# Two-layer transformer kernel: in the second layer's rounds the small steps stand behind the scores and maxima, directly ahead of the value products

## What is computed

```python
x = layernorm(x + L0_attn(x))   # 8 heads of 128, 2 key/value groups from a latent of 32, causal
x = layernorm(x + L0_ffn(x))    # silu(gate)*up, operands quantised to FP4 in blocks of 16
x = layernorm(x + L1_attn(x))   # 16 heads of 8, 4 key/value groups, not causal
x = layernorm(x + L1_ffn(x))    # 8 experts, softmax gate, gates under 0.1 dropped
# L1_attn
q = (x @ Wq.T + bq).reshape(b, n, G, hpg, HD); k, v = ...
scores = einsum('bqghd,bkgd->bghqk', q, k) / sqrt(8)
y = einsum('bghqk,bkgd->bqghd', softmax(scores), v) @ Wo.T + bo
```

## Time and profile before

| | us |
|---|---|
| median of 3 runs | 1475.09 (1474.76 to 1475.23) |
| the profiled execution | 1470.66 |
| its span | 1468.9 |
| second layer's rounds in it, until the last one ends | 631.8 to 1430 |

### The profile page before, as it was taken

How to read it: one execution, slowest core, us unless ns; L and a number is a source line. 1 busy time by engine, 2 the same in 40 slices (tenths; PEclk the granted TensorE clock), 3 DMA queues, 4 the chain that set the end, 5 groups by cost and what they waited for, 6 DMA issues and landing times.

```text
span 1468.9 us, 19049 instructions
## 1 busy us (share of the span) xinstructions
PE 1311.4 (89%) x6337; PEld 563.3 (38%) x6337; DVE 1088.7 (74%) x2289; ACT 845.8 (58%) x1621; POOL 110.8 (8%) x227
## 2 busy tenths in 40 slices
PE   4688889889999965899999999999999999999884
PEld 3354445344443432433333333333433333333322
DVE  3677696688645668778888788888879888987324
ACT  2445535554555421177777666777666776777660
POOL 2010010001010100000000002000110000000033
PEclk9669899899999975689999999999999999999897
DMA  3000000000000000000000000000000000000000
GB/s 100 1 1 1 1 1 1 0 1 1 1 1 1 0 1 0 1 1 1 2 1 1 1 1 9 1 1 1 1 1 8 1 1 2 1 1 1 1 8 8
DMA packets 9010, 6.13 MB, mean 4 GB/s; under 512 B 2184, under 2 KB 8272, under 8 KB 8912
## 3 DMA queue, kind: packets, MB, share of 16 engines
q1 hardware_dynamic: 8912, 4.91, 1.2%
HBM read 3.66 MB, written 1.05 MB: 3 GB/s over the span
## 4 chain that ended last, share of the span: by engine, by line
PE 71%; DVE 15%; ACT 7%; issue 4%; POOL 1%; DMA 1%; SPq 1%; DVEq 0%; POOLq 0%; ACTq 0%
PE ps L749 24%; PE ps L730 16%; PE ps L650 8%; DVE MP L1161 7%; PE ps L726 6%; ACT PR L926 4%; PE ps L655 4%; PE ps L646 2%; PE ps L712 2%; ACT QO L825 1%; PE ps L661 1%; PE ps L679 1%; DVE ps L1158 1%; PE ps L615 1%; PE ps L690 1%
## 5 line engine op out<-in xcount | busy, mean ns | idle before, releaser
L926 ACT ACTIVATE PR<-ps 128x512 f32<-128x512 f32 (+2 forms) x1344 | 699.1, 585 | 414.1 <-PE ps L730 224.3
L1161 DVE TENSOR_REDUCE MP<-ps 128x1 f32<-128x512 f32 x1216 | 764.2, 682 | 133.9 <-PE ps L650 87.4
L749 PE MATMUL ps<-PR,V 128*32 128x512 f32 (+2 forms) x2688 | 435.6, 605 | 0.7 <-ACT OS L825 0.7
L730 PE MATMUL ps<-Q,KO 64*128 64x512 f32 x1024 | 363.1, 466 | 26.6 <-ACT PR L926 20.6
L650 PE MATMUL ps<-KO,Q 64*128 64x512 f32 x1024 | 354.5, 447 | 16.3 <-DVE MP L1161 12.2
L730 PEld LDWEIGHTS ps<-Q,KO 64*128 64x128 f32 x1024 | 153.6, 186 | 350.3 <-ACT PR L926 290.3
L650 PEld LDWEIGHTS ps<-KO,Q 64*128 64x128 f32 x1024 | 164.4, 191 | 85.0 <-DVE MP L1161 47.9
L726 PE MATMUL ps<-QO,KO 97*128 97x512 f32 (+3 forms) x320 | 144.7, 464 | 21.2 <-ACT PR L926 18.8
L655 PE MATMUL ps<-KO,QO 96*128 96x512 f32 (+2 forms) x320 | 127.9, 441 | 19.5 <-DVE QO L1137 13.7
L749 PEld LDWEIGHTS ps<-PR,V 128*32 128x32 f32 (+1 forms) x2688 | 74.1, 116 | 130.6 <-issue 60.4
L726 PEld LDWEIGHTS ps<-QO,KO 97*128 97x128 f32 x320 | 62.8, 201 | 152.0 <-ACT PR L926 97.0
(11 more groups left out here) (179 smaller groups left out, 748.7 us busy)
## 6 DMA issues: line engine op xcount, KB each, us to landing
Q<-MR SPq DMA_DIRECT2D x64, 2.0 KB
result<-V SPq DMA_DIRECT2D x4, 256.0 KB, 2.3
H<-in_L_attn_wq SPq DMA_DIRECT2D x1, 512.0 KB, 6.7
HQT<-in_L_attn_wo SPq DMA_DIRECT2D x1, 512.0 KB, 5.0
ew<-in_L_ffn_expert_w SPq DMA_DIRECT2D x1, 512.0 KB
bq<-in_L_attn_bq SPq DMA_DIRECT2D x12, 0.1 KB
wd<-in_L_ffn_w_down SPq DMA_DIRECT2D x1, 176.0 KB, 3.7
wg<-in_L_ffn_w_gate SPq DMA_DIRECT2D x1, 128.0 KB, 4.4
```

What stands on the lines that cost most here:

```text
L730: m = nc.tensor.matmul(dst[:, :], KO1[rows, g, kt * P:(kt + 1) * P], Q1[rows, it, h // 2, :], start=True, stop=True)
L749: nc.tensor.matmul(dst, VO[layer][:, kt, g, :], PR[:, u % NP_RING, q0:QC], start=kt == 0, stop=kt == key_tiles(layer, c) - 1).then_inc(pv_ ...
L926: nc.scalar.activation(PR[:, u % NP_RING, q0:QC], ps[:, 8 - nb + u % nb, q0:QC], ACT.Exp, scale=SCALE[layer]).then_inc(exp_done, 1)
L1161: v.tensor_reduce(MP[:, buf, h, q, kc:kc + 1], bank[:, 0:w], AX, ALU.max).then_inc(free, 1)
```

## The change

The finished list passes through one more function before it is padded. It looks at each stretch from the first score of a round (head 0) of the second layer to that round's products. In it scores, maxima and the copies of finished results (`out_copy`) keep their order; any other step is held back, and put directly ahead of the products. A bankless step stays where it is as long as nothing is held, and is held too once something is. The first layer's rounds are left as they were. 66 of the second layer's 256 rounds come out in another order.

```diff
+        def beside_products(steps):
+            ends, end = [], False
+            for step in reversed(steps):
+                if step[0] == "products":
+                    end = step[1] in (1,)
+                ends.append(end)
+                if step[0] == "scores" and step[6] == 0:
+                    end = False
+            ends.reverse()
+            out, held = [], []
+            for step, end in zip(steps, ends):
+                kind = step[0]
+                if kind == "products" or not end:
+                    out += held + [step]
+                    held = []
+                elif kind in ("scores", "max", "out_copy") or kind in BANKLESS and not held:
+                    out.append(step)
+                else:
+                    held.append(step)
+            return out + held
-        program = padded(program)
+        program = padded(beside_products(program))
```

## The result

The changed kernel takes 1496.65 us (median of 4 runs, 1494.86 to 1507.12) against 1475.16 on the same chip (1474.76 to 1475.24): +21.5 us. The forecast was 1488.1, or +13.0. A second set of runs gave 1499.9 (1495.89 to 1511.68) against 1473.65 (1470.15 to 1479.98): ratio 1.0183, interval 1.0149 to 1.0216. So the sign was right and the size too small. The profiled execution is the longest of its set, 1507.12, and that of the second set, 1511.68, is too; that of the kernel before, 1470.66, is a short one.

The account below looks back on a forecast made before the run. PE bounds the second layer, with slack only before the fourth score; DVE bounds the end of a chunk's second iteration. Terms 1.8 + 0.0 + 6.0 - 0.3 + 0.5 + 5.0 = +13.0 gave 1488.1 us; range +9 to +16, with B and C 1479 to 1496.

Parts of the forecast that it names:

- The head and the tail: Second-layer round: first to fourth score, 1.18 us with PE slack; what follows the fourth score, 1.42 us with none.
- the five iterations forecast as 0.0: Third and fourth iterations of chunks 1 and 2, second of chunk 3: `out1` +0.23, `q1` -0.43, `shift` +0.20, sum 0.0.
- nine rounds at 0.5 and more: Last iteration, no maxima: two-expert rounds +0.7 and `gwT` rounds +0.5; nine rounds of this kind, +5.0 us.
- rival C: Granted clock falls to 1.2 GHz behind new PE waits at six places, about 1 us each: +19, 1494 us; chance 0.12.
- six new waits for ACT: Six places where the change adds a PE wait of about a microsecond, each costing about 1 if the clock falls.
- `stats`: Second iteration of chunks 1 and 2: POOL's sum 1.2 us later in its round, DVE waits 2.0; +1.8 a chunk.
- The first iteration of chunk 3, -0.3: `on1` directly behind `out1` waits for DVE's division, +0.9; a freed `q1` stall and DVE's list give back -1.2.
- The stall that was to be freed: Chunk 3, first iteration: DVE standing still at an early `q1`'s bank; its end, with DVE's list, gives -1.2.
- A: Rival for all 66 rounds: PE gains from fewer changes of form, heads shrink; -14, 1461 us; chance 0.07.
- B: Rival: DVE's total work bounds chunks 1 and 2, their 6.0 shrink to 0.5; +7.5, 1482.6 us; chance 0.17.
- D: Rival: heads and tails even out, only half the last iteration's cost remains; within 3 us; chance 0.06.
- the three things that would have proved it wrong: Heads below 1.18; `y1` earlier than 3.0 into its round; first chunk's `out1` rounds not longer than before.

Follow-up runs that it names:

- the waits filled: Changed kernel plus four unused 512-column matmuls ahead of each wait of `y1` and `logits` for ACT's copy: 1492.76 us, ratio 1.0134 against the kernel before.
- the last heads filled: Changed kernel plus one 512-column matmul between third and fourth score in each of the last iteration's 16 rounds: 1490.8 us, ratio 1.0118 against the kernel before.
- the repetition: The changed kernel timed again, unaltered, on a second chip against the kernel before: 1499.9 us, ratio 1.0183.
- both fillings: Changed kernel plus added matmuls ahead of the `y1` and `logits` waits and between third and fourth scores of the last iteration: 1495.02 us, 1.0131 against the kernel before.

## Why the prediction was too low

**The head and the tail: right.** Round by round at full clock:

| round | before | forecast | after |
|---|---|---|---|
| `q1` moved out of the head, first chunk | 3.37 | 3.65 | 3.66 |
| the same with maximum 1 or 3 unpaired | 3.60 | 3.88 | 3.89 |
| the round behind an early `q1` | 3.27 | 2.60 | 2.60 |
| `q1` with maximum 0 | 4.08 | 3.65 | 3.66 |
| `out1` | 3.14 | 3.37 | 3.42 |
| `shift` | 2.61, 2.84 | +0.20 | 2.81, 3.04 |
| `on1` and `y1` | 4.44 | 5.2 | 5.27 |
| last iteration, two experts | 3.97 | 4.70 | 4.52 |
| last iteration, `gwT` | 2.61 | 3.14 | 3.13 |
| last iteration, one expert | 3.13, 3.65 | | 3.66 |

Small misses: `out1` takes 0.59 of the tail, not 0.54, and the round behind it 0.07 more, so that the five iterations forecast as 0.0 became +0.12 to +0.18 each. The two-expert round was taken 0.18 too long, and an expert round of 3.65 grew by nothing, so that nine rounds at 0.5 and more were too many.

**The sum by stretches, in the profiled executions** (low: us at 1.2 GHz, before and after; these two lie further apart than the medians, and the measured column adds up to +35):

| stretch | forecast | measured | low |
|---|---|---|---|
| first chunk | +1.8 | +4.2 | 0, 5.6 |
| first iteration of chunk 1 | +1.2 | +5.6 | 3.4, 13.7 |
| second of chunk 1 | +1.8 | +2.7 | 0, 3.4 |
| first of chunk 2 | +1.2 | +3.9 | 0, 6.8 |
| second of chunk 2 | +1.8 | +2.7 | 0, 3.4 |
| first of chunk 3 | -0.3 | +3.8 | 3.4, 10.2 |
| third of chunk 3 | +0.5 | +0.5 | 0, 0 |
| last | +5.0 | +11.0 | 10.2, 26.7 |
| five others | 0.0 | +0.1 to +0.2 each | 0, 0 |

Where no low clock was added, the forecast holds. In the traces with the waits filled and with the last heads filled, the first chunk came to +2.0 and +2.1 for 1.8 and the first iteration of chunk 2 to +1.3 for 1.2, without low clock. The 5.6 us of the first chunk are the end of a stretch at 1.2 GHz that began in the first layer (608.9 of the profile after), which the change leaves alone; no term and no rival had that. Of the whole, the timed runs of the changed kernel give +13.1 to +15.8 at like clock, and 13.0 was forecast for the order.

**The step that failed** is the one that gave the clock no term in the sum and stood it apart as rival C: "If each brings such a stretch, each costs about 1: +19, 1494. 0.12." The price was too low, the places too few, the chance too small. *Price:* I took it from one block of products that took 1.93 instead of 1.06. The stretch does not end with that block: behind `logits` it takes in a whole `q1` round, +2.4 (6.07 for 3.66). *Places:* I counted six new waits for ACT, of which four exist, since in two cases the copy's writer stands a round ahead of the reader. I did not count `stats`, where my own working had DVE standing still for 2.0 us and PE therefore at a bank, nor the last iteration, whose heads I had emptied in the same paragraph. That place alone brings 16.5 us more at 1.2 GHz and, alone in a kernel, +11.7 us for a forecast of +5.0. *Chance:* showed a fall behind a wait of PE in the kernel before. 33.8 us more at 1.2 GHz in the whole kernel, at 0.32 to 0.39 us each, are 11 to 13 us of the 26.2 in the repetition. The measured +21.5 lies beside C's +19, but of the 53 us more at 1.2 GHz in the profiled execution only 24 lie in the first iterations of chunks 1 to 3, where C looked for them. The Trainium skill, "TensorE: Matmul & The Clock Gate", section "A second HAM failure mode: psum-queue depth-cycling", says that small frequent idles of PE between groups of matmuls can make the clock swing between its levels; the last iteration of the changed kernel agrees, with 6.97 us of idle in 65.65 us of rounds against 3.57 in 54.60, but in the one with the waits filled 6.09 us of the same small idles in 42.70 brought no fall. The same page's Terms price a us at the lower level at half a us; the two slopes used here are 0.32 and 0.39. Why they are lower was not tested.

What stays open is the cause of each single fall. That the changed kernel spends more time at 1.2 GHz than before, and is slower by it, is shown by the timed runs, by rounds of the same instructions that take 3.66 or 6.07, and by the kernels in which added work made it faster.

**The first iteration of chunk 3, -0.3: wrong in sign, the clock aside.** +3.8 less 6.8 x 0.39 leaves +1.1. The wait of on1 for DVE came as forecast: its round, 4.08 before, lasts 4.98 at full clock in the kernel with both fillings, +0.90 for +0.9. The stall that was to be freed came back one round later: the round that lasted 5.38 fell to 2.61, and the next rose from 3.28 to 5.39.

**`stats`: right in mechanism.** The sum starts 4.13 into the round of the last expert; 2.67 + 1.2 = 3.9 was expected. DVE idles 1.96 for the expected 2.5. Less the clock (3.4 x 0.39) the iteration is +1.4 for 1.8.

**A, B and D** are out. No head of the trace is shorter than 1.18, so fewer changes of form brought no round under the sum of its pieces; the 0.42 from the fourth score to the next form stays in every round. B's 6.0 us did not shrink, and D's 3 us are far off. Of the three things that would have proved it wrong, the heads and the `out1` rounds show nothing; `y1` starts before 3.0 only in chunk 3 (1264.85 - 1262.93 = 1.92), where its copy is written a round ahead. But one of its expectations failed, and it is the one that points at the clock: PE's busy time did not stay within a few us, it rose by 16.4.

## What to carry to other kernels

Put a small step where the engine waits anyway, in front of the instruction that has to wait; placed behind it, it was paid for in full here. When a change empties PE's idle places or adds waits, look at the granted clock of the rounds behind each such place, price a low stretch by the longest round that can fall into it, and put that in the sum and not beside it. A kernel without slack on PE can pay twice for idle time, once as a wait and again as slower work. And compare single rounds in more than one trace before giving a fall a cause: the same rounds ran at full clock in one execution and at 1.2 GHz in another.

## What the runs showed of the hardware

- Waits of PE of 0.7 to 1.9 us were followed by 3.4 to 6.8 us at 1.2 GHz (the falls at 1059.5 and 1127.7 of the profile after). The longer one, at `stats`, was followed by a fall in all ten cases of the five traces that have the whole change; the wait of 0.69 us at `logits` only in 5 of 8, and the same `q1` round took 6.07 us in one trace and 3.66 in another.
- Kernels with matmuls that compute nothing of use were faster than the one without: by 9.1 us with 16 of them in the last iteration (1499.9 to 1490.8), and by 7.1 with those ahead of `y1` and `logits`. Both together, on another chip, came to +21.2 against before, no better than either.
- With the same wait of 2.84 us for a DMA, at the start of the last iteration, PE stood at 1.2 GHz for 6.8 to 17.1 us, by the kernel. With 2.41 us of idle PE that iteration had 15.0 us at the lower level, with 3.94 us of idle 6.0. What sets the length is open.
